# Attention scores in ten visits per unit instead of twelve, with finer projection parts dealt by a table

## The reference

```python
q1, q2, k, v = (split_heads(x @ W) for W in (Wq1, Wq2, Wk, Wv))   # 16 heads of 32
q = concat([q1, q2])            # 32 query heads; each key and value head serves two
scores = einsum('bhqd,bhkd->bhqk', q, repeat(k, 2)) / sqrt(32)
p = softmax(where(causal, scores, min))
y = einsum('bhqk,bhkd->bhqd', p, repeat(v, 2))
y = y[:, :16] - sigmoid(x @ Wlam) * y[:, 16:]
out = y @ Wo
```

## Time and profile before

| | |
|---|---|
| runs, median (lowest, highest) | 2034.17 us (2033.46, 2034.27) |
| the profiled execution | 2035.76 us |
| its span, first to last instruction | 2034.0 us |
| mean granted TensorE clock | 0.995 |
| PE busy | 1962.1 us, 96% |
| DVE, POOL, ACT busy | 1305.1, 864.2, 827.7 us |

### The profile page before, as it was taken

One profiled execution on the slowest core, in us unless ns is written; L12 is line 12 of the kernel. 1 busy time (PEld: TensorE's weight loads), 2 busy tenths in 40 slices (PEclk: granted clock), 3 DMA queues, 4 the chain that ended last, 5 costly groups with the idle time before them and its releaser, 6 DMA issues.

```text
span 2034.0 us, 36832 instructions
## 1 busy us (share of the span) xinstructions
PE 1962.1 (96%) x15143; PEld 834.2 (41%) x15184; DVE 1305.1 (64%) x2610; ACT 827.7 (41%) x1259; POOL 864.2 (42%) x451
## 2 busy tenths in 40 slices
PE   7898999899999999999999999999998899899999
PEld 3444444444444443333333333333333334344444
DVE  5878686846847456566666666666667635774644
ACT  4435353425444322444434443344434452543431
POOL 3756576700000000667677667777776740000000
PEclk9999999999999999999999999999999999999999
DMA  8111010030000003000101010010000211000001
GB/s 243 32 31 33 30 42 27 21 140 1 1 1 1 1 1 76 23 17 23 22 22 22 12 26 14 22 23 22 2 22 6 60 36 42 1 1 22 21 0 42
DMA packets 71592, 60.21 MB, mean 30 GB/s; under 512 B 37312, under 2 KB 55744, under 8 KB 71168
## 3 DMA queue, kind: packets, MB, share of 16 engines
q1 hardware_dynamic: 64512, 45.27, 8.0%
q10 hardware_dynamic: 6912, 12.59, 2.0%
HBM read 43.02 MB, written 10.62 MB: 26 GB/s over the span
## 4 chain that ended last, share of the span: by engine, by line
PE 53%; DVE 5%; POOL 2%; issue 1%; ACT 1%; DVEq 0%; POOLq 0%; ACTq 0%
PE psum L128 9%; PE psum L1231 8%; PE psum L1321 8%; PE psum L1379 6%; PE psum L1362 6%; PE psum L152 5%; PE psum L1271 3%; PE psum L1335 2%; PE psum L1358 2%; POOL b_totals L1628 1%; PE psum L1349 1%; DVE b_maxima L1701 1%; PE psum L1280 1%; DVE psum L1709 1%; DVE x L1767 0%
## 5 line engine op out<-in xcount | busy, mean ns | idle before, releaser
L1628 POOL TENSOR_TENSOR b_totals<-b_totals,b_probs 128x2048 f32<-128x2048 f32 (+3 forms) x100 | 323.9, 3239 | 151.7 <-ACT b_probs L1546 148.1
L1709 DVE CUSTOM_DVE_ANT_0 psum<-psum,b_rest 128x512 f32<-128x512 f32 (+3 forms) x512 | 233.7, 526 | 172.2 <-PE psum L1321 172.0
L447 PE MATMUL psum<-hT,a_win 128*128 128x512 f32 x640 | 292.9, 601 | 2.6 <-DVE a_parts L751 1.2
L128 PE MATMUL psum<-hT,b_early 128*128 128x512 f16 x1024 | 227.2, 381 | 9.8 <-DVE b_middle L214 6.9
L128 PE MATMUL psum<-hT,W 128*128 128x512 f16 x1024 | 227.5, 382 | 3.7 <-DVE a_win L214 3.6
L1546 ACT ACTIVATE b_probs<-psum 128x1024 f32<-128x1024 f32 (+3 forms) x214 | 153.6, 768 | 150.5 <-PE psum L1362 150.4
L1701 DVE TENSOR_REDUCE b_maxima<-psum 128x2 f32<-128x1024 f32 x128 | 150.9, 1221 | 86.0 <-PE psum L1321 85.7
L1628 POOL TENSOR_TENSOR b_totals<-b_totals,b_rest 128x2048 f32<-128x2048 f32 (+3 forms) x50 | 161.9, 3238 | 68.3 <-ACT b_rest L1546 66.6
L447 PEld LDWEIGHTS psum<-hT,a_win 128*128 128x128 f32 x640 | 120.2, 192 | 130.8 <-issue 129.5
L128 PEld LDWEIGHTS psum<-hT,b_early 128*128 128x128 bf16 x1024 | 100.0, 98 | 133.8 <-DVE b_middle L214 8.8
L128 PEld LDWEIGHTS psum<-hT,W 128*128 128x128 bf16 x1024 | 100.7, 99 | 126.4 <-issue 7.0
(11 more groups left out here) (244 smaller groups left out, 3476.6 us busy)
## 6 DMA issues: line engine op xcount, KB each, us to landing
a_parts<-in_w_guT ACTq DMA_DIRECT2D x32, 256.0 KB, 2.7
ternary<-W SPq DMA_DIRECT2D x1, 6144.0 KB, 18.3
a_win<-in_w_inT SPq DMA_DIRECT2D x20, 256.0 KB, 7.9
a_parts<-in_w_pT ACTq DMA_DIRECT2D x16, 256.0 KB, 2.6
b_down<-lam_rows SPq DMA_DIRECT2D x32, 128.0 KB, 2.7
b_early<-ternary SPq DMA_DIRECT2D x8, 512.0 KB, 8.9
out<-x SPq DMA_DIRECT2D x16, 256.0 KB, 2.3
x<-in_x SPq DMA_DIRECT2D x3, 1024.0 KB, 8.0
```

The lines of the kernel that those rows point to most:

```text
L128: last = pe.matmul(self.bank[self.up_bank(i, m) + part], self.gu[:, k * 2 * HID + col:k * 2 * HID + col + P], self.hT[:, at:at + BLK], sta ...
L447: last = pe.matmul(ring(s, j), win[:, at:at + P], core["hT"][:, (i * KT + k) * BLK:(i * KT + k + 1) * BLK], start=(k == 0), stop=(k == KT ...
L1628: pool.tensor_tensor(acc, acc, held(u, s)[:, :, off:BLK], ALU.add).then_inc(summed, 1)
L1709: last = dve.tensor_tensor_reduce(scores, scores, row_mask[:, BLK - width:BLK], 1.0, -3e38, ALU.add, ALU.max, maxima[u % 2][:, at:at + 1])
```

## The change

Three things change at once, all in the attention.

1. **Ten visits.** `STEPS` keeps its 12 steps, in a slightly different order, and `VISITS` groups them. Visit 1 holds the steps of 384 and 128 queries of chunk 0 side by side in one PSUM pair, visit 8 those of chunk 1. All masks of a visit come first; both steps are weighed in the next visit. ACT's `exps` waits for the buffers of all steps of a visit before its first exponential.
2. **Rows in visits 0 to 8** (`FIRST_ROW = 0`), in another order.
3. **Parts.** k, q and v jobs have 8 parts of 256 columns. They are dealt one after the other by two tables, some ahead of the visit's row (places 0 and 1), some behind it (places 3 to 5). den stands at (2, 2), right behind the row of visit 2 and ahead of that visit's part, and at (4, 4), behind that visit's part. neg and both out jobs of a unit stand in visit 9. norm jobs 0 to 3 move to visits 3, 5, 6 and 7, behind the rows.

```diff
-STEPS = [(c, kt) for c in range(CQ) for kt in range(TPB * (c + 1))]
+STEPS = [(0, 0), (0, 1), (0, 3), (0, 2)] + [(1, kt) for kt in (0, 1, 2, 3, 4, 5, 7, 6)]
+VISITS = [[0], [1, 2], [3], [4], [5], [6], [7], [8], [9, 10], [11]]
-ROWS = [[(0, 0), (2, 0)], [(4, 0)], [(1, 0), (5, 1)], [(5, 0)], [(6, 0)], [(4, 1), (6, 1)], [(3, 0)], [(7, 1)], [(7, 0)]]
+ROWS = [[(4, 0)], [(5, 0)], [(0, 0), (2, 0)], [(1, 0), (5, 1)], [(3, 0)], [(4, 1), (6, 1)], [(6, 0)], [(7, 1)], [(7, 0)]]
-FIRST_ROW = 1
+FIRST_ROW = 0
...
-PARTS = {"k": KT, "q": KT, "v": KT}
-FIRST_HALF = {(0, 0): "k0", (2, 1): "den1", (3, 0): "k1", (5, 1): "den0", (6, 0): "q0", (8, 0): "q1", (10, 1): "neg0"}
-SECOND_HALF = {(0, 0): "q0", (2, 1): "den1", (3, 0): "q1", (5, 1): "den0", (6, 0): "v0", (8, 0): "v1", (10, 1): "neg0"}
-OUT_AT = [{9: 2, 11: 3}, {10: 0, 11: 1}]
-FILL_BEFORE_ROWS = (0, 4)
-NORM_AT = {(3, 0): 0, (4, 0): 1, (6, 0): 2, (7, 0): 3}
-INVERT_AT = {3: (1, 0), 4: (1, 1), 6: (0, 0), 7: (0, 1)}
+PARTS = {"k": 2 * KT, "q": 2 * KT, "v": 2 * KT}
+MADE_IN = [("k0", "k1", "q0", "q1"), ("q0", "q1", "v0", "v1")]
+AHEAD_OF_ROWS = {0: 2, 1: 1, 3: 2, 4: 1, 5: 1, 6: 1, 7: 1, 8: 1}
+BEHIND_ROWS = {0: 3, 1: 2, 2: 1, 3: 3, 4: 1, 5: 3, 6: 3, 7: 3, 8: 3}
+PLACES = 6
...
+    FILLS[-1].update({(2, 2): "den1", (4, 4): "den0", (9, 2): "neg0"})
+OUT_AT = [{9: (2, 3)}, {9: (0, 1)}]
+NORM_AT = {(3, 3): 0, (5, 3): 1, (6, 3): 2, (7, 3): 3}
+INVERT_AT = {3: (1, 0), 4: (1, 1), 5: (0, 0), 6: (0, 1)}
...
-            def project(weights, r, c, k, to):
-                at = ((r // HT * CQ + c) * KT + k) * BLK
+            def project(weights, r, c, part, to):
+                k, width = part % KT, BLK // 2
+                first = part // KT * width
+                at = ((r // HT * CQ + c) * KT + k) * BLK + first
                 for own in COLUMNS:
-                    last = pe.matmul(to[own, :], weights[:, k * P + own.start:k * P + own.stop], hT[:, at:at + BLK],
-                                     start=(k == 0), stop=(k == KT - 1))
+                    last = pe.matmul(to[own, first:first + width], weights[:, k * P + own.start:k * P + own.stop],
+                                     hT[:, at:at + width], start=(k == 0), stop=(k == KT - 1))
...
+                    for place in range(PLACES):
+                        if place == 2 and row_in(u, i):
+                            row(*row_in(u, i))
+                        if (u, i, place) in PART_AT and (place or u < UNITS - 1):
+                            fill(*PART_AT[u, i, place])
+                    for out_of in out_in(u, i):
+                        output(*out_of)
...
-            def exps(u, s):
...
+            def exps(u, i):
+                for s in VISITS[i]:
+                    c, kt = STEPS[s]
+                    g = u * NS + s
+                    if kt == 0:
+                        if u:
+                            act.wait_ge(filled, NTH[("den", u - 1, c)] + 1)
+                    elif summed_by(u, s) > len(prob):
+                        act.wait_ge(summed, min(summed_by(u, s) - len(prob), ALL_SUMS))
+                        act.wait_ge(weighed, g - len(prob) + 1)
                 for a in range(2):
```

More of the change, by code:

```diff
@@ L939, in job_from @@
     if u == UNITS - 1:
[L940 to L941 removed]
+        return {(1, 1): ("den", u - 1, 1), (3, 0): ("den", u, 0)}.get((i, place))
+    name = FILLS[w].get((i, place), "none0")
     kind, n, last = name[:-1], int(name[-1]), r == TURNS - 1
@@ L964 @@
 EPILOGUE_BANKS = [7]
[L966 removed]
 PART_AT, ENDING, STEADY = {}, {}, []
[L968 removed]
+for _at in itertools.product(range(UNITS), range(NV), range(PLACES)):
     _job = job_from(*_at)
     if _job:
[L971 to L976 removed]
+        if not STEADY or STEADY[-1] != _job:
+            STEADY.append(_job)
+            _part = 0
+        PART_AT[_at] = (_job, _part)
+        _part += 1
+        if _part == PARTS.get(_job[0], 1):
+            ENDING[_at] = _job
 JOBS = PROLOGUE + STEADY + EPILOGUE
@@ L996, in out_in @@
     r, w = divmod(u, 2)
-    return (r - 1 + w, OUT_AT[w][i]) if i in OUT_AT[w] and 0 < r + w < TURNS else None
+    return [(r - 1 + w, two) for two in OUT_AT[w].get(i, ()) if 0 < r + w < TURNS]
 OUTS = [(r, two) for r in range(TURNS - 1) for two in range(QT // 2)]
@@ L1002 @@
 for _u in range(UNITS):
-    for _i in range(NS):
+    for _i in range(NV):
         PAIR_USES += [("score", _u, _i, a) for a in range(2)]
@@ L1006 @@
             PAIR_USES += [("row", *row_in(_u, _i), a) for a in range(2)]
-        if out_in(_u, _i):
-            PAIR_USES.append(("out", *out_in(_u, _i), 0))
+        PAIR_USES += [("out", *_out, 0) for _out in out_in(_u, _i)]
 PAIR_NTH = {use: n for n, use in enumerate(PAIR_USES)}
@@ L1266, in fill @@
                     pe.wait_ge(wv_loaded, 16)
-                    t = 2 * two + part // 2
-                    for k in (part % 2 * 2, part % 2 * 2 + 1):
-                        at = ((b * CQ + t // TPB) * KT + k) * BLK + t % TPB * P
-                        for own in COLUMNS:
-                            last = pe.matmul(to[own, t % 2 * 2 * P:(t % 2 + 1) * 2 * P],
-                                             hT[:, at + own.start:at + own.stop],
-                                             wv_all[:, k * D + h * P:k * D + (h + 2) * P],
-                                             start=(k == 0), stop=(k == KT - 1))
+                    t, k = 2 * two + part // KT, part % KT
+                    at = ((b * CQ + t // TPB) * KT + k) * BLK + t % TPB * P
+                    for own in COLUMNS:
+                        last = pe.matmul(to[own, t % 2 * 2 * P:(t % 2 + 1) * 2 * P],
+                                         hT[:, at + own.start:at + own.stop],
+                                         wv_all[:, k * D + h * P:k * D + (h + 2) * P],
+                                         start=(k == 0), stop=(k == KT - 1))
                 elif kind == "den":
@@ L1337, in output, with scores @@
                 last.then_inc(out_done, 1)
-            def scores(u, s):
-                c, kt = STEPS[s]
+            def scores(u, i):
+                steps = VISITS[i]
+                c, kt = STEPS[steps[0]]
                 r, w = divmod(u, 2)
-                off, diagonal = step_width(s), kt >= TPB * c
+                diagonal = kt >= TPB * c
                 to = []
@@ L1554, in _ @@
             for u in range(UNITS):
-                for i in range(NS):
+                for i in range(NV):
                     exps(u, i)
@@ L1563, in _ @@
                         act.activation(e_root[:, :], e_var[:, :], ACT.Sqrt).then_inc(early_root, 1)
-                    for place in range(2):
+                    for place in range(PLACES):
                         if (u, i, place) in ENDING:
                             copy_out(ENDING[u, i, place])
+                        if place == 0 and CHUNK_LAST[0] in VISITS[i - 1]:
+                            weigh_out(u, 0)
             weigh_out(UNITS - 1, 1)
@@ L1818, in _ @@
             for u in range(UNITS):
-                for i in range(NS):
-                    if u == UNITS - 2 and NORM_AT.get((i + 1, 0), 2) < 2:
-                        early_turn(0, NORM_AT[i + 1, 0])
-                    if i == NS - 2 and u + 1 < UNITS:
+                for i in range(NV):
+                    if u == UNITS - 2 and NORM_AT.get((i + 1, 3), 2) < 2:
+                        early_turn(0, NORM_AT[i + 1, 3])
+                    if i == NV - 1 and u + 1 < UNITS:
                         negate(u + 1)
```

130 lines of the change are left out of this document (57 added, 73 removed).

## The result

The changed kernel's median is 2043.03 us (2042.50 to 2044.66, 5 runs) against 2034.17 (2033.46 to 2034.27, 5 runs as well): a ratio of 1.0045 with a 95% interval of 1.0031 to 1.0060, so it is slower, by 0.45%. The forecast was 2044.3. The profiled execution took 2043.03 us, span 2041.2, mean granted clock 0.996.

What follows compares the result with a forecast made beforehand. PE's instruction order was taken as the bound. Units 1 to 12 +7.0, unit 0 +1.5, unit 13 +0.5, units 14 and 15 +1.5, start -0.4: +10.1 on 2034.17 gives 2044.3 us, range 2033 to 2052.

Steps and rivals of the forecast that it cites:

- the likeliest case: The forecast itself, 2044.3 us, slower than before: chance 0.61, own range 2038 to 2050.
- main term: Visits 2 and 4: PE waits for ACT's copy of bank 7 between adjacent jobs, 0.90 us, twice a unit.
- neither wait was saved: Two rivals on bank 7: copies cost no more than they cover, 2026 (0.12); only one wait paid, 2035 (0.13).
- POOL was not the bound: Rival: POOL's chain of sums, take and spread becomes the bound, +9 to +10, 2054 us; chance 0.12.
- the weight loads did not show: Rival: 1536 added weight loads in projections are exposed, 42 us, 2086 us; chance 0.02.
- Waits that stay or come: Steady unit: 0.35 stays at row 1, about 0.36 each comes behind rows 3 and 5; bank-7 waits add 1.80.
- Halved parts cost nothing: Projections: 256-column instructions run as fast as 512-column ones, doubled weight loads stay hidden; nothing in the sum.
- The switches: PE between column and row strips: two visits less save 0.56 a unit, finer dealing returns 0.17, net -0.39.
- Unit 0, +1.5: Unit 0: waits of 5.7 us against 3.85 before, with the switches +1.5 us.
- Unit 13, +0.5: Unit 13: later rows stay uncovered, two bank waits come, DVE's extra statistics hurt less: +0.5 us.
- Unit 14: Visit 8 stalls some 6 us behind POOL's second early row; last bias 2.5 later, unit 15 regains 1.0: +1.5.
- Tail: zero: Work behind the last unit, with DMA queues and first phase: no change.

Runs made afterwards that it cites:

- experiment 1: Changed kernel with ACT copying bank 7 out twice for the 27 jobs that have a neighbour right behind them on the bank: 2062.06 us.
- experiment 2: Changed kernel with ACT copying bank 7 out twice for the 57 other projection, value and den jobs of the units: 2046.55 us.
- experiment 5: Changed kernel with den moved to (2, 0) and (4, 3), other rows of visits 0 to 8 given one half part ahead, three behind: 2030.96 us.
- experiment 6: Kernel before the change, each k or q projection part issued as two times 8 instructions of 256 columns instead of 8 of 512: 2035.75 us.
- experiment 4: Changed kernel with den of the unit before moved ahead of the row of visit 2, nothing else moved: 2051.28 us.
- experiment 3: Changed kernel with the part behind the row of visit 4 moved behind the row of visit 2, den staying behind visit 4's row: 2045.00 us.
- experiment 11: Changed kernel with DVE's scaled-variance instruction in unit 13 removed, ACT's square root reading the variances itself with scale and bias: 2044.68 us.

## Why the prediction was right

Sign and size were right, 1.3 us off the median, inside the likeliest case's own range. Its main term was right by its mechanism: 0.92 a wait measured, 0.90 predicted, 27 of them, and experiments 1, 2 and 5 show it as the cause. Of the rivals, neither wait was saved (experiment 1 made both grow by the copy), POOL was not the bound (no idle time ahead of the first bias in units 2 to 13, 0.49 us in unit 14), and the weight loads did not show (experiment 6). Point by point:

- *Waits that stay or come*: 0.345 behind rows 3 and 5 (0.36), 0.385 at the mask (0.35), in unit 0 1.21 (1.15) and 2.67 (2.60). Right.
- *Halved parts cost nothing*: right, in experiment 6. There the rule of the Trainium skill, page "TensorE: Matmul & The Clock Gate", section "Part 3: Packing small matmuls — row/col tiling", that a weight load overlaps matmuls in flight only where its row group differs, is not borne out: 1536 more loads changed nothing. The same section names a second case, loads into a background weight buffer; whether these loads were such, no run shows.
- *The switches*: -0.39 a unit was a little too small. A row behind a part costs 0.217 and not 0.229, a first half part behind a row 0.152 and not 0.157; with the steady unit at +0.44 in place of +0.58 this is the 1.7 us of units 1 to 12.
- *Unit 0, +1.5*, came to +2.0. "Its other waits are 0.35, 0.36, 0.36 and 0.90" left out the row of visit 0, which waits 0.69 for an exponential.
- *Unit 13, +0.5*, was mis-sized: +2.0. The step "DVE's extra statistics hurt less" failed. One of them landed in a sum of POOL, below.
- *Unit 14*: the stall came where it was put, by the mechanism named (POOL's second early row behind norm 1), at 6.35 us of idle time for "some 6". Its cost in all was less: unit 14 +2.2 for +2.5, unit 15 -1.8 for -1.0. The sum had no term for the clock. It was down for 6.8 us in unit 14 of both kernels, so that this cancels; that it did is luck.
- *Tail: zero*: -1.7 came. Behind unit 15 the kernel before had PE's clock down for 3.4 us after PE had been idle for 2.9, the changed one had not, after the same idle time. No term of the sum could hold this.

Of the spans' +7.2, so, the terms were 4.9 too high and 2.0 too low. That the median came within 1.3 is partly luck: the profiled execution of the kernel before was 1.6 above its median, that of the changed one on it.

## What to carry to other kernels

An engine that takes its instructions in order pays the whole hand-over (here 0.07 + 0.60 + 0.05, and 0.2 of lost overlap) wherever two jobs on one buffer stand next to each other; put a piece of other work as long as the copy between them, and check that what stood there is not missed elsewhere: a wait can itself be the cover of another, and taking it away alone (experiment 4) made the kernel slower. Before carrying a wait's size to a new place, look at which job its releaser works on. And judge a small edit by the stretch it touches: the medians of experiments 2, 3, 4 and 11 lie some 3 to 7 us above what the edited places account for.
